# Feed-forward: the first row of a half's down products waits block by block for the split activations

## The reference

```
x = fwht(layernorm(x) * SU_ug) / 64                    # Walsh-Hadamard transform
up   = x @ W_up.T   * (Wscale_ug[:2048] * 64)          # 512 -> 2048
gate = x @ W_gate.T * (Wscale_ug[2048:] * 64)
a = silu(gate) * up
a = fwht(a * SU_dp) / 64
y = a @ W_down.T * (Wscale_dp * 64)                    # 2048 -> 512
x = x + 0.5 * y
```

## Time and profile before

| | |
|---|---|
| median of 3 runs | 2294.91 us |
| profiled execution | 2296.02 us |
| its span | 2294.2 us |
| TensorE matmul busy | 2006.6 us, 87% |
| VectorE busy | 1268.6 us, 55% |
| ScalarE busy | 726.7 us, 32% |
| GpSimd busy | 258.7 us, 11% |
| mean granted TensorE clock | 0.923 |

### The profile page before, as it was taken

One profiled execution on the slowest core, in us unless ns is written; L12 is line 12 of the kernel. 1 busy time (PEld: TensorE's weight loads), 2 busy tenths in 40 slices (PEclk: granted clock), 3 DMA queues, 4 the chain that ended last, 5 costly groups with the idle time before them and its releaser, 6 DMA issues. The chain is left out here.

```text
span 2294.2 us, 29080 instructions
## 1 busy us (share of the span) xinstructions
PE 2006.6 (87%) x11854; PEld 944.4 (41%) x11854; DVE 1268.6 (55%) x2323; ACT 726.7 (32%) x1131; POOL 258.7 (11%) x236
## 2 busy tenths in 40 slices
PE   4784868887862999999999999989998999999998
PEld 3442333333332444444444444444444444444443
DVE  5777457576566554545574356626574456533322
ACT  4562132332412222232253223522343234412211
POOL 3630222312200000001000100001000100000000
PEclk7986778988865999999999999999999999999999
DMA  7224030211322222221111111111111111122321
GB/s 259 92 74 172 0 60 17 44 43 18 58 77 75 83 92 92 100 75 38 47 65 37 57 45 56 56 55 37 38 65 37 65 53 50 56 101 101 116 102 58
DMA packets 87680, 158.71 MB, mean 69 GB/s; under 512 B 44342, under 2 KB 51324, under 8 KB 82812
## 3 DMA queue, kind: packets, MB, share of 16 engines
q1 hardware_dynamic: 85244, 152.14, 20.3%
q0 software_dynamic: 2304, 4.72, 0.9%
HBM read 128.52 MB, written 18.87 MB: 64 GB/s over the span
## 5 line engine op out<-in xcount | busy, mean ns | idle before, releaser
L1184 PE MATMUL ps<-arena 128*128 128x512 f16 (+1 forms) x4512 | 1015.5, 380 | 22.6 <-DVE arena L1989 12.9
L1184 PEld LDWEIGHTS ps<-arena 128*128 128x128 f16 x4512 | 435.3, 99 | 543.2 <-issue 48.3
L1934 PE MATMUL ps<-arena 128*128 128x512 f16 x1536 | 349.0, 383 | 29.5 <-DVE arena L1980 16.3
L1934 PEld LDWEIGHTS ps<-arena 128*128 128x128 f16 x1536 | 147.4, 98 | 207.4 <-issue 29.4
L1989 DVE SCALAR_TENSOR_TENSOR arena<-arena,ps 128x512 f32<-128x512 f32 x128 | 87.9, 686 | 210.0 <-ACT arena L1956 209.3
L1956 ACT ACTIVATE arena<-ps,arena 128x512 f32<-128x512 f32 x128 | 87.6, 684 | 362.1 <-PE ps L1184 362.0
L2541 ACT ACTIVATE arena<-ps 128x1024 f32<-128x1024 f32 (+3 forms) x128 | 90.1, 704 | 254.5 <-PE ps L2450 254.5
L2646 DVE CAST arena<-arena 128x1024 f16<-128x1024 f32 (+3 forms) x128 | 66.2, 517 | 150.5 <-ACT arena L2541 148.5
L2612 DVE TENSOR_REDUCE arena<-ps 128x2 f32<-128x256 f32 (+3 forms) x128 | 99.6, 819 | 65.1 <-PE ps L2394 65.1
L2017 DVE SCALAR_TENSOR_TENSOR arena<-ps,arena 128x512 f32<-128x512 f32 x64 | 44.0, 687 | 139.6 <-PE ps L1934 139.4
L1998 DVE SCALAR_TENSOR_TENSOR arena<-ps,arena 128x512 f32<-128x512 f32 x128 | 95.7, 748 | 39.2 <-PE ps L1184 39.1
(11 more groups left out here) (268 smaller groups left out, 2436.2 us busy)
## 6 DMA issues: line engine op xcount, KB each, us to landing
arena<-wug_dram SPq DMA_DIRECT2D x128, 512.0 KB, 3.3
arena<-wd_hi_dram SPq DMA_DIRECT2D x16, 1024.0 KB, 5.0
arena<-wd_lo_dram SPq DMA_DIRECT2D x16, 1024.0 KB, 7.2
wug_dram<-arena SPq DMA_DIRECT2D x4, 2048.0 KB, 15.1
arena<-arena SPq DMA_DIRECT2D x72, 64.0 KB, 2.9
arena<-arena POOLq DMA_DIRECT2D x72, 64.0 KB, 2.7
arena<-_attn_hidden_states_dram SPq DMA_DIRECT2D x4, 1024.0 KB, 11.8
arena<-in_L_ffn_W_up_dram SPq DMA_DIRECT2D x8, 512.0 KB, 4.8
```

What stands on the lines that cost most here:

```text
L1184: ins = pe.matmul(out, left[a](c), right[b](c), start=(at == 0), stop=(at == 3 * n - 1))
L1934: ins = pe.matmul(k.ps[:, bank, :], act[x][:, slot, cols], wd[y][:, f, :], start=(f == 0 and m == 0), stop=(f == 7 and m == 2))
```

## The change

In `feed_tensor`, the first down row (u = 0) of each half waited for the low parts of all 8 blocks of its half. Now it waits at first for those of the first four; in its second unit, ahead of the three matmuls of each of the blocks 4 to 7, it waits for the low part of that block. The other rows, the order of the instructions and the other engines are as before.

```
--- before.py
+++ after.py
@@ -1913,7 +1913,7 @@
                     turn_tensor(k, pe, index, c, SOLO_TURN[c])
         if u == 0:
             pe.wait_ge(s["down_in"], 32 * (2 * q + half + 1))
-            pe.wait_ge(s["f_lo"], FB * q + 8 * (half + 1))
+            pe.wait_ge(s["f_lo"], FB * q + 8 * half + 4)
         if half and woven:
             if u == 0:
                 pe.wait_ge(s["f_prod"], FB * (q + 1))
@@ -1930,6 +1930,8 @@
     act, wd = (k.act_hi, k.act_lo), (k.wd_hi, k.wd_lo)
     for f in range(4 * part, 4 * part + 4):
         slot = (FB * q + 8 * half + f) % ACT_SLOTS
+        if u == 0 and f >= 4:
+            pe.wait_ge(s["f_lo"], FB * q + 8 * half + f + 1)
         for m, (x, y) in enumerate(((0, 0), (0, 1), (1, 0))):
             ins = pe.matmul(k.ps[:, bank, :], act[x][:, slot, cols], wd[y][:, f, :], start=(f == 0 and m == 0),
                             stop=(f == 7 and m == 2))
```

## The result

The changed kernel takes 2272.18 us (median of 6 runs, 2269.53 to 2275.99), the kernel before 2295.27 (6 runs, 2293.59 to 2296.39): a ratio of 0.9901 with a 95% interval of 0.9888 to 0.9913, 23.1 us faster. The forecast was 2272.8 in a range of 2269 to 2279.5.

The account below looks back on a forecast made before the run. TensorE was taken to bound the kernel, so its stalls at down rows count fully. Stalls 17.2 plus clock 5.5 minus 0 for added waits gave 22.7 us, hence 2272.8 us, range 2269 to 2279.5.

Parts of the forecast that it names:

- That TensorE's stalls are the kernel's time: From about 1738 us the chain is almost pure TensorE, so a microsecond standing still at a down product is a kernel microsecond.
- The stalls: Idle time of TensorE ahead of first down rows at nine places; cutting it was to save 17.2 us.
- the solo ones: Half 1 of q = 0, 1, 6 and 7: whole idle time goes, 1.66 us for the first three and 2.28 us.
- q = 0 half 0: First down row there waits for its bank, freed by `L1989`, and starts at 800.98 instead of 801.58: 0.60 us.
- the three woven ones: Half 1 of q = 2, 3 and 4: the row starts once `L1998` frees the bank, 3.32 us each, 9.96 in all.
- nine late rows: First down rows of a half where TensorE stood idle, 20.2 us together; the prediction put seven in second halves.
- the upper bound for the added waits: If TensorE stopped at each of 64 added waits for the shortest stop, 0.53 us, they would cost 34 us.
- The clock: Half clock behind the stalls of q = 2, 3 and 4 was to vanish with them, giving back 5.5 us.
- The added waits at nothing: The 64 added waits in the middle of accumulations were taken to cost zero and to stall nowhere.
- The wait did not move: Rival: the output product or last block ends the wait in woven passes instead, leaving 2290.4 us; chance 0.03.
- The clock rival: Clock loss stays or an equal one comes up elsewhere; only the stalls go, 2277.7 us; chance 0.13.
- the toll: Rival: each added wait exposes one weight load of 0.10 us, 6.4 us in all, 2279.2 us; chance 0.04.

Follow-up runs that it names:

- the filled wait: Kernel before, its woven half 1 still waiting for all 8 low parts, with 13 unread matmuls put into that wait: 2290.15 us, ratio 0.9978.
- the woven halves alone: Changed kernel with the new waits only in half 1 of passes q = 2 to 5, the other halves waiting as before: 2278.09 us, ratio 0.9927.
- The repeated run: The changed kernel unaltered, run again as partner for later experiments on the same chip: 2274.41 us, ratio 0.9916 against the kernel before.

## Why the prediction was right

**That TensorE's stalls are the kernel's time** held. From the first down row's start to the end of the span it was 2294.2 - 801.58 = 1492.6 us before and is 2267.8 - 797.91 = 1469.9, 22.7 less, and the stall ahead of that row adds 0.56.

**The stalls**, forecast at 17.2 us: the solo ones went as worked out (0.53 + 0.60 + 0.53 + 2.28), q = 0 half 0 gave 1.76 - 1.20 = 0.56 for a forecast of 0.60, the three woven ones 3.77 - 0.50 = 3.27 each for 3.32, q = 5 gave 3.18 - 0.50 = 2.68 for 2.73. Together 17.0 us. The small excess of the forecast has one cause: between `L2000`'s end (1231.73 + 0.75 = 1232.48) and TensorE's start lie 0.15 us, where I had taken the 0.10 seen behind `L1980`.

What the forecast missed is that a stall that goes wholly is worth more than its idle time. The row of q = 0, half 1, started 864.93 - 862.49 = 2.44 us after its transposes did, and now starts 860.55 - 858.81 = 1.74 after them:

```profile
862.49 1.91 PE L1851 MATMUL ps<-arena 128*128 128x128 f32 x16
...
858.81 1.91 PE L1851 MATMUL ps<-arena 128*128 128x128 f32 x16
860.55 1.68 PE L1936 MATMUL ps<-arena 128*128 128x512 f16 x7
```

That is 0.70 us for an idle time of 0.53. It is 0.76 in q = 1 and 0.70 in q = 6, and in q = 7 the stretch from the start of half 0 to the start of half 1 is 2.45 us shorter, for 2.28. These four places give 4.6 us in place of 3.9, and the stalls 17.7 in all, 0.5 over the forecast.

Three readings in the prediction are off and bear on no term of the sum. Eight of the nine late rows, not seven, are of a second half. The shortest stop ahead of a down row is 0.35 us, behind `L2017` in q = 5, not 0.53; the upper bound for the added waits would be 22 us with it, not 34. And the instructions that stand ahead of the high part on ScalarE (`L2557`, `L2559`, `L2567`) are no evictions: they are the logarithm, the exponential and the copy of the attention's normalised output, from and to `arena`. ScalarE is idle for 0.82 us between the second and the third, while the last product had been ready since 1237.69 us:

```profile
1239.05 0.63 ACT L2567 ACTIVATE arena<-arena 128x512 f16<-128x512 f32 x1 [0.82 <-DVE arena L2669]
```

So the written order of ScalarE made the last high part late, as the order of VectorE made the additions late. Making it earlier was not tried.

**The clock**, forecast at 5.5 us: the three first units run at 1.00, and the filled wait, which keeps the stalls, measured 4.95 us (3.2 to 7.1), 5.6 between the profiles behind the first row. The choice to count it wholly was right. What it does not have is a fixed size. q = 5 kept its clock through 3.18 us, and q = 7 kept it behind 2.28 us in the profiles of the kernel before and of the filled one and lost it in that of the woven halves alone, so the clock's part of the gain can vary from run to run by about 1.7 us a place.

**The added waits at nothing** held, with 384 more to show it. The Trainium skill (Advanced Engine Details and Errata, section Network/Comms) gives 50 to 100 ns for reading a semaphore's value from a sequencer. At 50 ns in the open the 384 waits would have cost 19 us, an estimate from that figure, and the measured chain shows none. Whether a wait is no such read or the matmuls under way hide it, these runs can't tell.

**The sum**: by the profiles 17.7 + 5.5 = 23.2 us, for a forecast of 22.7 and a measured 23.1. That the two agree to 0.1 is partly luck, since the interval of the ratio is 20 to 26 us; the firmer check is the 22.7 + 0.56 = 23.3 us above, between the profiles from the first changed stall on. Between the two profiled executions it is 26.4 us; 3.1 of them lie ahead of the first changed row, which came idle at 801.58 - 1.76 = 799.8 us before and at 797.91 - 1.20 = 796.7 after. The change does nothing there. The repeated run came to that point at 799.60 - 1.20 = 798.4, so this part is variation between executions. Taking one profile from the other would have given the change 3 us that are not its own.

**The rivals.** The wait did not move: it would have shown ahead of the second unit or of the output product, and neither has idle time. The clock rival and the toll are excluded by the windows and the chain above. Two stretches of half clock remain in the woven stage after the change, as two were there before outside the changed places. That of q = 2 is still there; the other has moved to another pass:

```profile
1695.60:1699.00 3.40, 3.40 (x10) 1.06 (x10) 1.87 (x8) 0.00 (x0) 0.00 (x0) 0.51 0.00 0
```

It stands in q = 4, where there was none, and the one of q = 3 is gone. All stand behind the same 1.76 or 1.77 us of idle time at `L1184`, which q = 2, 3 and 4 all have. A further one, which the prediction does not count, stands in q = 1 behind 3.64 us of idle time at `L1184`, before and after.

What the prediction did not say is that four waits are not needed: one ahead of the second unit gives the same.

## What to carry to other kernels

A wait that stands ahead of a whole accumulation should stand ahead of the first matmul that reads the data; on an engine that sets the end, every microsecond of it counts, and a satisfied wait inside the accumulation cost nothing that could be measured between matmuls 0.217 us apart. Price a stall of TensorE with the clock of the work behind it, read in a window, since here a fifth of the gain was that. Where a stall goes wholly, measure from start to start: it was worth 0.16 us more than its recorded idle time. And when a stall goes, read what releases the next one: here it was not data but the order of two additions on VectorE, worth half as much again.

## What the runs showed of the hardware

13 matmuls whose result nobody reads, put into a wait of 3.3 us, kept TensorE at 2.4 GHz and made the kernel 4.95 us faster without shortening a wait. Stalls of one length don't always cost the clock: 3.77 us did in three of three places, 3.18 us did not, 2.28 us did once and did not at two other times, and 1.76 us at `L1184` did in two of three passes in both kernels' profiles and in all three in the repeated run's. Over all nine profiles it is 20 of 27 places, while 3.64 us at `L1184` in q = 1 did in all nine.

384 satisfied waits more in the middle of accumulations left 96 matmuls at 20.79 us. A stall's recorded idle time leaves out 0.16 us: places with 0.95 us of it gave back 1.11 us from start to start, and those with 0.53 gave back 0.70.
